# Attention products in two-part float32r stacks of 64 rows instead of six-part bf16 stacks of 96

## The reference

```python
qkv = (x @ qkv_w.T + qkv_b).reshape(B, L, 3, H, D).transpose(2, 0, 3, 1, 4)
q, k, v = qkv[0], qkv[1], qkv[2]
q, k = apply_rotary(q, cos, sin), apply_rotary(k, cos, sin)
attn = softmax(einsum('bhqd,bhkd->bhqk', q, k) * D ** -0.5)
out = einsum('bhqk,bhkd->bhqd', attn, v)
x = x + out.transpose(0, 2, 1, 3).reshape(B, L, C) @ proj_w.T + proj_b
```

## Time and profile before

| what | value |
|---|---|
| runs | 1560.33, 1560.25, 1558.60 us (median 1560.25) |
| the profiled execution, its own time | 1559.88 us |
| its span | 1558.1 us |
| TensorE matmul busy | 1304.5 us (84%) |
| VectorE busy | 1141.7 us (73%) |
| ScalarE busy | 770.9 us (49%) |
| Pool busy | 364.6 us (23%) |
| mean granted clock | 0.88 of full |
| `project_qkv` | 0 to 198 us |
| `attend`, maxima of the first group alone | 198 to 243 us |
| `attend`, the 16 groups | 243 to 1020 us |
| `cross_attend` and `experts` | 1020 to 1558 us |

### The profile page before, as it was taken

One profiled execution on the slowest core, in us unless ns is written; L12 is line 12 of the kernel. 1 busy time (PEld: TensorE's weight loads), 2 busy tenths in 40 slices (PEclk: granted clock), 3 DMA queues, 4 the chain that ended last, 5 costly groups with the idle time before them and its releaser, 6 DMA issues. The chain is left out here.

```text
span 1558.1 us, 22119 instructions
## 1 busy us (share of the span) xinstructions
PE 1304.5 (84%) x7000; PEld 626.6 (40%) x7000; DVE 1141.7 (73%) x2540; ACT 770.9 (49%) x984; POOL 364.6 (23%) x332
## 2 busy tenths in 40 slices
PE   5777488999999999999999999957888411799995
PEld 3444212222222222222222222246777410689894
DVE  6788487889888898788988889127677478676751
ACT  2333203666666666666666666923444200455552
POOL 3777530000000000000000000012322201376754
PEclk9888657999999999999999999977678555799998
DMA  3246482113231133302333000041322110153532
GB/s 116 92 146 194 157 185 55 28 39 62 59 62 28 39 62 58 63 11 58 62 59 61 9 5 7 8 149 54 111 81 70 46 52 0 35 162 93 158 89 27
DMA packets 100871, 111.19 MB, mean 71 GB/s; under 512 B 24992, under 2 KB 77984, under 8 KB 99744
## 3 DMA queue, kind: packets, MB, share of 16 engines
q1 hardware_dynamic: 94624, 101.50, 25.0%
q0 software_dynamic: 6144, 8.39, 2.9%
HBM read 71.73 MB, written 37.75 MB: 70 GB/s over the span
## 5 line engine op out<-in xcount | busy, mean ns | idle before, releaser
L623 DVE TENSOR_REDUCE b_max_halves<-banks 128x1 f32<-128x512 f32 x1024 | 635.7, 682 | 83.2 <-PE banks L678 70.6
L591 ACT ACTIVATE b_probs<-banks 128x1024 f32<-128x1024 f32 x512 | 496.4, 1021 | 314.4 <-PE banks L736 313.2
L678 PE MATMUL banks<-b_k,b_q 96*128 96x512 bf16 x1024 | 354.8, 401 | 31.7 <-DVE b_identb L644 17.5
L736 PE MATMUL banks<-b_q,b_k 99*128 99x512 bf16 x1024 | 302.1, 382 | 1.7 <-DMA b_q<-b_max_rows 0.2
L703 PE MATMUL banks<-b_probs,b_v 128*32 128x512 f32 x2048 | 274.5, 608 | 0.5 <-ACT b_probs L591 0.5
L678 PEld LDWEIGHTS banks<-b_k,b_q 96*128 96x128 bf16 x1024 | 85.1, 97 | 410.9 <-DVE b_max_halves L623 350.8
L607 POOL TENSOR_SCALAR b_minus_max<-b_max 128x32 f32<-128x32 f32 x16 | 4.6, 288 | 742.2 <-DVE b_max L627 742.2
L736 PEld LDWEIGHTS banks<-b_q,b_k 99*128 99x128 bf16 x1024 | 94.1, 98 | 108.7 <-ACT b_probs L591 55.6
L359 PE MATMUL banks<-a_w,a_xnT 128*128 128x512 f32 x128 | 74.5, 712 | 1.2 <-issue 1.2
L703 PEld LDWEIGHTS banks<-b_probs,b_v 128*32 128x32 f32 x2048 | 40.4, 108 | 82.9 <-issue 82.1
L1538 DVE TENSOR_TENSOR e_hTl<-e_hT,e_hTh 128x512 fp32r<-128x512 f32 x64 | 43.6, 688 | 41.1 <-ACT e_hT L1346 41.1
(11 more groups left out here) (215 smaller groups left out, 1742.0 us busy)
## 6 DMA issues: line engine op xcount, KB each, us to landing
e_w<-in_w SPq DMA_DIRECT2D x16, 1024.0 KB, 9.0
v_tiles<-a_v SPq DMA_DIRECT2D x8, 1024.0 KB, 6.0
b_v<-v_tiles SPq DMA_DIRECT2D x16, 512.0 KB, 9.5
q_stacks<-a_parts SPq DMA_DIRECT2D x24, 256.0 KB
k_stacks<-a_parts SPq DMA_DIRECT2D x24, 256.0 KB
b_q<-q_stacks SPq DMA_DIRECT2D x16, 384.0 KB, 4.8
b_k<-k_stacks SPq DMA_DIRECT2D x16, 384.0 KB, 7.8
a_x<-in_x SPq DMA_DIRECT2D x8, 512.0 KB, 4.6
```

Source lines behind the costliest of these rows:

```text
L591: nc.scalar.activation(pr[:, u, s % 2], ps[:, 2 * u:2 * u + 2, :], ACT.Exp, scale=D ** -0.5).then_inc(s_ex[u], 1)
L623: v.tensor_reduce(mxp[:, par].rearrange("p j t h -> p (j t h)")[:, k:k + 1], ps[:, bank(last), :], AX.X, ALU.max).then_inc(s_mr, 1)
L678: nc.tensor.matmul(ps[:, bank(m), :], qs[g][0:RQ, j, P * t:P * t + P], ks[g][0:RQ, j, CH * kh:CH * kh + CH], start=True, stop=True).then_i ...
L736: ins = nc.tensor.matmul(ps[:, j, :], ks[g][0:RQ + 3, j, P * (s % KT):P * (s % KT) + P], qs[g][0:RQ + 3, j, CH * (s // KT):CH * (s // KT) ...
```

## The change

q and k are written as two float32r parts instead of three bf16 parts, the leading and the trailing one. A head's stack is 48 rows of three pairs (leading.leading, leading.trailing, trailing.leading). It lies in 64 partitions: 48 rows of data, rows 48 to 62 zero, row 63 with the row maximum against minus one. Two heads lie one above the other in the 128 partitions, so that their products use different halves of the array's rows; head pairs 0 and 1 of a group are two planes of the tile.

In `project_qkv` lines 215, 276 and 327 go away; VectorE writes the trailing part directly. The stacks in DRAM are float32, 32 rows for a head instead of 48 of bf16. `store_qk` waits once for all four column sets and then issues 8 DMAs of 512 KB. A group is loaded with 9 DMAs instead of 7.

In `attend` the unit is a half-group: 4 heads, 512 queries, eight steps. Each step has four maximum products (PER = 4), two between the pairs of scores and two behind the values, and they run 12 steps ahead of the scores (AHEAD = 48). Before the first scores only 48 maxima run alone, and the row maxima of the first half-group are sent after 32. The row maxima are not split: TensorE turns them in float32, ScalarE copies them, and four DMAs put them in place for each half-group. The turned output is copied to SBUF by ScalarE, inverted there by VectorE and scaled by Pool. New at the start: Pool clears the rows 32 to 63 and 96 to 127 of all stacks (16 memsets of 32 partitions x 2048 float32, of which 12 are in `attend`), and DMAs put the rows of minus one.

```diff
@@ project_qkv
             def store_qk(i):
+                sp.wait_ge(s_pb[1], 4 * i + 4)
                 for f in range(4):
-                    sp.wait_ge(s_pc[f % 2], 4 * i + 2 + f // 2 + 1)
-                    for m in range(3):
+                    for m in (1, 0):
                         dst = (qst, kst)[f // 2][i][8 * (f % 2):8 * (f % 2) + 8, 16 * m:16 * m + 16, :]
-                        sp.dma_start(dst, parts[:, f, m, :]).then_inc(s_qs[f], 16)
+                        sp.dma_start(dst, parts[:, f, m, :].bitcast(F32)).then_inc(s_qs[f], 16)
...
-                act.wait_ge(s_r, 8 * i + 4 * h + f + 1)
-                nc.scalar.activation(parts[:, f, 1, half], rest[:, f % 2, :], ACT.Copy).then_inc(s_pb, 1)
...
-                v.tensor_tensor(parts[:, f, 2, half], rest[:, 1, :], parts[:, f, 1, half], ALU.subtract)\
-                    .then_inc(s_pc[1], 1)
+                v.tensor_tensor(parts[:, f, 1, half], ps[:, 6 + q, :], parts[:, f, 0, half], ALU.subtract)\
+                    .then_inc(s_pb[q], 1)
...
+def clear_pad(g, pool, a, s, n):
+    for r in range(2):
+        g.memset(a[HR * r + RZ:HR * r + HR, :, :].bitcast(F32), 0.0).then_inc(s, 1)
+        pool.wait_ge(s, n + r + 1)
...
+    for s in range(2):
+        heads = slice(G * g + s, G * g + G, 2)
+        for dst, src, runs in ((q, qst, ((0, 0, 16), (16, 0, 32))), (k, kst, ((0, 0, 32), (32, 0, 16)))):
+            for to, lo, n in runs:
+                sp.dma_start(dst[HR * s + to:HR * s + to + n, :, :].bitcast(F32),
+                             src[b][heads][:, lo:lo + n, :].rearrange("h r n -> r h n")).then_inc(s_ld, 16)
@@ attend
+            for hg in range(NH):
+                for kt in range(KT):
+                    places = [[], [], [], []]
+                    for x in range(PER):
+                        k = PER * (KT * hg + kt) + AHEAD + x
+                        if not (last and k >= MAXS):
+                            places[1 if x < 2 else 3].append(("max", k))
+                    if kt == 2 and not (first and hg == 0):
+                        places[2].append(("out", hg - 1))
+                    if kt == AHEAD // PER - KT and not (last and hg == NH - 1):
+                        places[3].append(("rows", hg + 1))
...
+            for g in range(1, 3):
+                sp.wait_ge(s_clear[g], 4)
+                load(0, g)
+            sp.wait_ge(s_ra, 1)
+            rows(0, 0)
+            for g in range(1, NG):
+                ones(g)
             load_context_weights(sp, cw, s_cw, wts)
...
+                            if u == 0:
+                                for kind, k, m in late:
+                                    if kind == "rows":
+                                        rows(n["items"] + m, m)
+                                    else:
+                                        out(8 * i + k, k % 2, n["items"] + m, m)
+                                late = [x for place in range(4) for x in at[hg, kt, place] if x[0] != "max"]
...
+                stack = slice(HR * s, HR * s + RS)
+                at = CH * h + P * t
+                nc.tensor.matmul(ps[:, bank(m), :], qs[g][stack, p, at:at + P],
+                                 ks[g][stack, p, CH * kh:CH * kh + CH], start=True, stop=True).then_inc(s_mm, 1)
...
+                            for s in range(2):
+                                stack = slice(HR * s, HR * s + HR)
+                                ins = nc.tensor.matmul(ps[:, 2 * u + s, :], ks[g][stack, u, P * kt:P * kt + P],
+                                                       qs[g][stack, u, CH * h:CH * h + CH], start=True, stop=True)
+                            ins.then_inc(s_st[u], 1)
+                            if u == 0:
+                                ring(hg, kt, 1)
```

More of the change, by code:

```diff
@@ L336, in body @@
                         rotate(i, h, t)
-                        if t % 2 == 0 and not (first and h == 0):
-                            split(*away(i, h, -1), t)
             bodies(pool, body)
-            for f in range(0, 4, 2):
-                split(B - 1, 1, f)
         @block.tensor
@@ new lines, in plan, with count, taken, before @@
+            return at, items
+        START = [("max", k) for k in range(NB)] + [("rows", 0)] + [("max", k) for k in range(NB, AHEAD)]
+        def count(items, kinds):
+            return sum(kind in kinds for kind, _ in items)
+        def taken(items, m):
+            kind = items[m][0]
+            return (s_mr, count(items[:m + 1], ("max",))) if kind == "max" else \
+                (s_ra, count(items[:m + 1], ("rows", "out")))
+        def before(i, first):
+            n = {}
+            n["items"] = len(START) if first else len(plan(False, False)[1]) * i + len(START) - 1
+            n["max"] = AHEAD if first else MAXS * i + AHEAD
+            n["copied"] = 1 if first else 2 * NH * i
+            return n
@@ L541, in _ @@
             for s in stores[3]:
[L542 removed]
+                sp.wait_ge(s, 32 * B)
             def body(i, first, last):
[L545 to L566 removed]
+                items = plan(first, last)[1]
@@ new lines, in body @@
+                n = before(i, first)
+                for hg in range(NH):
+                    g, h = hg // 2, hg % 2
+                    if h == 0:
+                        if not (first and g == 0):
+                            sp.wait_ge(s_pv[1], 4 * (8 * i + hg))
+                        if not (last and g > 0):
+                            if g == 0:
+                                if first:
+                                    sp.wait_ge(s_clear[3], 4)
+                                load(i, 3)
+                            else:
+                                load(i + 1, g - 1)
+                    if not (last and hg == NH - 1):
+                        sp.wait_ge(s_ra, n["copied"] + taken(items, items.index(("rows", hg + 1)))[1])
+                        rows((hg + 1) // 2 % NG, (hg + 1) % 2)
+                    if not (first and hg == 0):
+                        sp.wait_ge(s_att, 8 * i + hg)
+                        if hg == 0:
+                            store(i - 1, NG - 1, 1)
+                        else:
+                            store(i, (hg - 1) // 2, (hg - 1) % 2)
@@ L593, in _ @@
             bodies(act, body)
-            take(8 * NG * B)
+            take(4 * NH * B)
+            m = len(plan(False, True)[1])
+            out(NH * B - 1, 1, before(B - 1, False)["items"] + m, m)
         @block.gpsimd
@@ L681, in rows @@
-            def rows(n, before, m):
-                pe.wait_ge(s_mp, n + 1)
-                free(before, m)
-                nc.tensor.matmul(ps[:, bank(m), :].bitcast(BF16)[0:3 * G * KT, 0:P],
-                                 mp[:].rearrange("p m j t -> p (m j t)"), identb[:],
-                                 is_transpose=True, start=True, stop=True).then_inc(s_mm, 1)
-            def outputs(half, before, m):
-                pe.wait_ge(s_oe, half + 1)
-                free(before, m)
+                    s, c = taken(items, m - NR)
@@ L691, in outputs, with rows @@
+            def rows(hg, n, items, m):
+                pe.wait_ge(s_mx, hg + 1)
+                free(n, items, m)
+                nc.tensor.matmul(ps[:, bank(m), 0:P], mx[:], ident[:], is_transpose=True, start=True, stop=True)\
+                    .then_inc(s_mm, 1)
+            def outputs(hg, n, items, m):
+                pe.wait_ge(s_oe, hg + 1)
+                free(n, items, m)
                 for t in range(NT):
@@ L714, in body, with ring @@
+            none = {"items": None, "max": 0, "copied": 0}
+            for m, (kind, k) in enumerate(START):
+                if kind == "max":
+                    maxima(k, none, START, m)
+                else:
+                    rows(k, none, START, m)
+            pe.wait_ge(s_one, 16 * 2 * NG)
             def body(i, first, last):
-                at = plan(first, last)[0]
-                def ring(g, s, place):
-                    for kind, k, m in at[g, s, place]:
+                at, items = plan(first, last)
+                n = before(i, first)
+                def ring(hg, kt, place):
+                    for kind, k, m in at[hg, kt, place]:
@@ L719, in ring @@
                         if kind == "max":
[L720 removed]
+                            maxima(k, n, items, m)
                         elif kind == "out":
[L722 removed]
+                            outputs(8 * i + k, n, items, m)
                         else:
[L724 to L729 removed]
+                            rows(8 * i + k, n, items, m)
```

368 lines of the change are left out of this document (163 added, 205 removed).

## The result

| | before | after |
|---|---|---|
| median | 1559.79 us (1558.60 to 1560.33, 4 runs) | 1637.47 us (1631.07 to 1641.99, 4 runs) |
| span of the profiled execution | 1558.1 us | 1637.9 us |
| first stage | to 197.9 | to 210.2 |
| first scores | 246.7 | 253.9 |
| last turned output of attention | 1018.4 | 1095.9 |

The change makes the kernel 5% slower: ratio 1.0496, 95% interval 1.0457 to 1.0535. The forecast of 1585 had the sign, and the time lies inside the range, but the loss is 78 us where 25 was said. The stages divide it: +12 in the first, -5 from the stage's start to the first scores, +70 from there to the last output, +2 behind.

What follows compares the result with a forecast made beforehand. The prediction took a loop through TensorE, VectorE and three ring banks as the bound. Attention +21, first half-group's row DMAs +3 and first stage +1 made +25 on 1559.9 us: 1585 us, range 1537 to 1655.

Steps and rivals of the forecast that it cites:

- my own case: Whole kernel: 1585 us, from 1555 with free weight loads to 1622 with 0.10 each and the first stage's upper bound; chance 0.52.
- the third rival: Attention: the array's halves do not work side by side; steps 3.05 us, output stalls 3 us, total 1653 us; chance 0.21.
- The steady step: Attention step with four maxima, bound by a loop through TensorE, VectorE and ring banks: 2.82 us, bounds 2.72 and 2.92.
- M3 to M2: Attention loop, from the first maximum product behind the values to the next step's second: 1.17 plus 0.05 for late weights.
- M2 to values: Attention loop, from the step's second maximum product through the second pair of scores to the value products: 0.23 plus 0.31, 0.54 us.
- values to M3: Attention loop, from the value products to the first maximum product behind them: 1.00 as now plus 0.05 late load, 1.05 us.
- the unexplained 0.85 per group: Attention: the old kernel's group takes 49.05 us where steps sum to 48.2; the other 0.85 was kept in every sum.
- the bound of -17: First stage: lower bound of its +1 us sum, if stores are not waited for and only the end is later.
- The start: Attention's start: from the stage's start to the first scores 34 us, with 50 as upper bound at 3.5 us a memset.
- Output and rows: Attention: turning the output, waiting for ScalarE's copy and row transposes add 2.6 us in each half-group.
- Hidden loads: Whole kernel: weight loads hidden and stores unwaited; step 2.72, half-group 24.2, total 1537 us; chance 0.19.
- VectorE as the bound: Attention: the ring loop hides and VectorE's reductions close the step; half-group 19.7, total 1417 us; chance 0.06.

Runs made afterwards that it cites:

- The bf16 run: Changed kernel with score and maximum products reading the same stacks through bf16 views, leaving out the low bits of both parts: 1572.64 us, ratio 1.0089.
- the runs without the second long step: Changed kernel with ScalarE copying the turned output behind the second Exp of the same step, not the next step's first: 1599.28 us, ratio 1.0257.
- with 2.70 us steps: Changed kernel with each step's second maximum product issued behind the second pair of scores, right ahead of the values: 1569.84 us, ratio 1.0072.
- the run with the row DMAs first: Combined, unrolled kernel with the four row DMAs ahead of the loads of groups 1 and 2 at attention's start: 1496.58 us against 1490.77 without.
- the kernel with the stacks on 16 engines: Combined, unrolled kernel with the two parts in separate DRAM planes, stores of 128 rows in one dimension, 13 load DMAs: 1479.93 us, ratio 0.9493.

## Why the prediction was right or wrong

Against the profiled execution's 1639.7 us the sum is 55 us short. The loop, its links and its two long steps were right; three terms of the sum were too small, and one cost was missing. The time lies inside the stated range only by luck: my own case ended at 1622, and the rest of the range came from the third rival, whose mechanism the trace refutes. By the sum's own steps:

- **The steady step: 0.05 for a late load should have been 0.10, twice.** That was the upper bound from the experts' rows, 0.49 against 0.39, and I talked it down with an argument no row had (a half stack loading beside the other half). The bf16 run and the 2.94 us steps show the full 0.10. It also stands elsewhere than I had it: a late load delays what follows its product, so M3's is in M3 to M2 (1.28 for 1.17) and M2's in M2 to values (0.67 for 0.54), and none is in values to M3 (0.99 for 1.00 as now). 2.935 for 2.82 in each of 244 steps: **+28 us**, the largest single part.
- **Low clock: no term at all.** From the first scores to the last step with maxima it is 813.6 us, by the full-clock pattern (25.98 us for a half-group, 30.5 of them) 792.4. The rest, 21, is low-clock stretches and the loop's turn, of which the unexplained 0.85 per group covered 13: **+8 us**. It goes with the stalls, though no run shows what makes it fall: the runs without the second long step, or with 2.70 us steps, have it only at the loop's turn, and without the hardware loop hardly at all (no step over 3.6 us).
- **Stores in the first stage: the waits were +33 and not +18.** With 16 engines and no wait for a store, ScalarE's last split ends 24.1 us before the unchanged kernel's (163.3 for 187.4): the relief of -25 was right. In the change it ends 9.1 behind it (196.5), so the waits cost 33; I had counted three of 6 us, where ScalarE waited twelve times, four in each of three batches, 63 us in all. Behind the last split the change needs 3.2 us more and not 8, since eight stores left the queue in 12 us and not in 21. Putting the old wait back gives 29.8 us back. That this comes out at -17.4, beside the bound of -17, is luck, as 34 us of ScalarE's waits remain in it. The stage ended at 210.2 where the sum had 198.9: **+11 us**.
- **The start: 34 us was 43.7, +10 us.** Maxima, memsets (1.80 each, estimate 1.8) and the queue's order were right. Missing was the way from issue to landing, 9.7 us in the median for the rows of minus one, and 9.4 us for four row DMAs behind a group load, where 2.5 is their own.
- **Row DMAs of the first half-group: +3 was 0** in the change. It appears only when the start is made earlier, in the run with the row DMAs first: 6.65 us.
- **Output and rows: right.** 2.6 us per half-group forecast; 3.95 + 3.80 + 3.53 is 2.46 above three steady steps, -4 us in all. The Trainium skill, "TensorEngine Tiling (Array Packing)" (Key Properties), lets TensorE drain at a change of tiling mode, which I had estimated at 14 us more. The trace shows none behind the turning: from its start to the scores it is 0.59 us (600.08 to 600.67), with transposes of 128 rows that start 0.11 to 0.16 apart and the score product of 64 rows 0.20 after the last, and the 0.09 more is what a late float32r load costs alone.
- **Rivals.** Halves not side by side (1653): refuted in the timeline, where the first pair of scores takes 0.39 in all; with both scores in one half they start 0.23 apart. The second pair does start 0.34 apart (357.81, 0.73 in all), but there M2 holds one half, as my own sum had it. This rival's time was nearest all the same, which shows that a time alone supports no mechanism. Hidden loads (1537): refuted by the 0.50 and by the waits for stores; 8 x 2.72 + 2.6 is 24.4 and not 24.2, so by its own terms its time is 1542. VectorE as the bound: not until the loop is shortened.

Together 28 + 8 - 4 for the steps, 11 + 10 - 3 for the stores, the start and the row DMAs, and 1 + 2 for the last output and the later stages: 53 of the 55.

The expected gain of the change, five maxima per step turned into four and a lighter VectorE, did not come since VectorE was never last alone. It was there to be had: the order of a few ring items, the place of one copy and one wait on SyncE turn +5.0% into -3.7%.

## What to carry to other kernels

Write a software pipeline's step as a loop of links before touching an engine's load, and put every product that waits for nothing into the link that waits: here moving one product behind two others was worth 68 us, with the same instructions. Give a late weight load of float32r its full 0.10 us, and give each stall a second price, since the granted clock can fall behind it. When one wait replaces several on a shared store queue, ask who reuses the buffer, and look first at how many DMA engines such a store moves on.

## What the hardware showed that was not expected

- With scores and maxima all in rows 0 to 63, TensorE was granted 0.51 in the mean of 1100 us while busy 97%; with the maxima on both halves and only the scores in one, it was granted 0.97 from 300 to 630 us and 0.91 from 700 to 920.
- Products in the two row halves start together (357.81 twice), also where one is a maximum of 63 rows and the other a score of 64. The Trainium skill, "TensorE: Matmul & The Clock Gate" (Part 3), has row groups start about 4 ns apart, and the trace agrees as far as its 10 ns show.
- A weight load of 128 float32r columns is 193 ns, of 128 bf16 columns with stride 2 94 ns.
- Four small DMAs of 2 KB took 2.5 us of SyncE's queue alone and 8.3 to 9.9 us at the start of attention, where a group load had been issued just before them (6.0 in the kernel with the stacks on 16 engines).
